# Macaron block with routed experts: combine weights gathered with the token rows, lists of token numbers only, expert 0's positions first, constants made early

## The reference, cut to what matters

```python
probs = softmax(xf @ router_w.T)                # 8192 tokens, 8 experts
topw, topi = top_k(probs, 2)
topw = topw / (topw.sum(-1, keepdims=True) + 1e-06)
# each expert keeps the 1280 tokens of its own with the largest weight (capacity)
order = lexsort((-fw, fe)); rank = arange(N * K) - starts[se]; keep = rank < capacity
g, u = disp @ wg, disp @ wu                     # per expert, 256 x 1024
eo = (silu(g) * u) @ wd                         # per expert, 1024 x 256
out = zeros.at[st].add(eo_of_the_token * (sw * keep))
x = x + 0.5 * mixture(layernorm(x))
```

## Time and profile before

| | |
|---|---|
| median of 3 runs | 1907.24 us (1907.22 to 1910.83) |
| the profiled execution's own time | 1911.83 us |
| its span, first to last instruction | 1910.1 us |
| TensorE matmul busy | 1622.9 us, 85% of the span |
| VectorE, ScalarE, GpSimd busy | 64%, 46%, 45% |
| mean granted TensorE clock | 0.937 |

### The profile page before, as it was taken

One profiled execution on the slowest core, in us unless ns is written; L12 is line 12 of the kernel. 1 busy time (PEld: TensorE's weight loads), 2 busy tenths in 40 slices (PEclk: granted clock), 3 DMA queues, 4 the chain that ended last, 5 costly groups with the idle time before them and its releaser, 6 DMA issues.

```text
span 1910.1 us, 40320 instructions
## 1 busy us (share of the span) xinstructions
PE 1622.9 (85%) x13943; PEld 1278.3 (67%) x13943; DVE 1231.0 (64%) x2915; ACT 886.9 (46%) x1627; POOL 869.0 (45%) x636
## 2 busy tenths in 40 slices
PE   4512999999999999986899751299999999999998
PEld 4411787877878788763577641168787787878876
DVE  8886748566485766526798887664745647465551
ACT  5521544445454454525565551144544545545452
POOL 5714163544626355136676651326254452635513
PEclk9999999999999999995899755589999999999999
DMA  6731261524516153126666450136062441615312
GB/s 220 261 133 40 83 128 41 129 53 95 120 29 148 32 116 66 18 42 166 143 146 146 139 197 0 28 95 127 28 143 47 102 105 43 132 39 125 61 23 28
DMA packets 261236, 182.16 MB, mean 95 GB/s; under 512 B 160938, under 2 KB 247860, under 8 KB 261172
## 3 DMA queue, kind: packets, MB, share of 16 engines
q1 hardware_dynamic: 230452, 139.37, 26.8%
q0 software_dynamic: 30720, 41.96, 13.3%
HBM read 89.01 MB, written 54.53 MB: 75 GB/s over the span
## 4 chain that ended last, share of the span: by engine, by line
PE 72%; DVE 12%; issue 6%; POOL 4%; DMA 2%; ACT 2%; SPq 0%; DVEq 0%; POOLq 0%; ACTq 0%
PE bank L1459 43%; PE bank L1472 22%; PE bank L1440 3%; POOL rstd L419 1%; DVE kT L1040 1%; DVE rT L1040 1%; POOL rows L423 1%; PE bank L1420 1%; PE bank L1504 1%; DVE gat L1249 1%; ACT xn L779 1%; DMA xs<-in_L_attn_x 1%; DVE v L1243 1%; DVE xn L944 1%; POOL hot_v L390 1%
## 5 line engine op out<-in xcount | busy, mean ns | idle before, releaser
L1459 PE MATMUL bank<-xT,w_g 128*128 128x320 f16 x3072 | 503.3, 300 | 31.4 <-DMA xT<-gat 31.4
L1115 DVE SCALAR_TENSOR_TENSOR unit_buf<-bank,sc_cur,unit_buf 128x320 f32<-128x320 f32 x512 | 281.6, 550 | 355.0 <-PE bank L1459 228.3
L1459 PE MATMUL bank<-xT,w_u 128*128 128x320 f16 x3072 | 503.3, 300 | 0.0
L721 ACT ACTIVATE unit_buf<-bank,sc_cur 128x320 f32<-128x320 f32 x512 | 269.5, 526 | 408.4 <-PE bank L1459 407.0
L1472 PE MATMUL bank<-w_d,xs 128*128 128x256 f16 x3840 | 423.8, 273 | 0.0
L1472 PEld LDWEIGHTS bank<-w_d,xs 128*128 128x128 f16 x3840 | 375.2, 98 | 44.4
L1459 PEld LDWEIGHTS bank<-xT,w_g 128*128 128x128 f16 x3072 | 295.6, 99 | 141.6 <-issue 31.9
L390 POOL TENSOR_TENSOR hot_v<-hot_b,val 128x400 bf16<-128x400 bf16 x128 | 147.7, 1154 | 520.8 <-DVE hot_b L1098 520.8
L1459 PEld LDWEIGHTS bank<-xT,w_u 128*128 128x128 f16 x3072 | 301.5, 98 | 118.1
L396 POOL DMA_INDIRECT gat<-rows_d,id_next x160 | 179.7, 1123 | 200.4 <-DVE id_next L1108 140.0
L1121 DVE TENSOR_TENSOR xs<-unit_buf,xs 128x320 f16<-128x320 f32 x512 | 268.4, 524 | 2.2
(11 more groups left out here) (230 smaller groups left out, 1811.9 us busy)
## 6 DMA issues: line engine op xcount, KB each, us to landing
rows_d<-rows SPq DMA_DIRECT2D x32, 512.0 KB, 3.4
raw_gu<-in_L_ffn_wg SPq DMA_DIRECT2D x16, 1024.0 KB, 5.6
raw_gu<-in_L_ffn_wu SPq DMA_DIRECT2D x16, 1024.0 KB, 9.1
raw_d<-in_L_ffn_wd SPq DMA_DIRECT2D x16, 1024.0 KB, 5.5
x_d<-xs SPq DMA_DIRECT2D x1, 8192.0 KB, 32.6
out_x<-xs SPq DMA_DIRECT2D x16, 512.0 KB, 3.5
xs<-in_L_attn_x SPq DMA_DIRECT2D x7, 1024.0 KB, 5.7
xs<-x_d SPq DMA_DIRECT2D x5, 1024.0 KB, 6.1
```

Source lines behind the costliest of these rows:

```text
L721: act.activation(act_s[:, u % 2, :], bank[u % 2][:, 0:CW], ACT.Silu, scale=sc_cur[:, 3:4]).then_inc(S.s_ready, 1)
L1115: dve.scalar_tensor_tensor(h32[:, u % HB, :], bank[2 + u % 2][:, 0:CW], sc_cur[:, 4:5], act_s[:, u % 2, :], mult, mult).then_inc(S.h32_rea ...
L1459: mm = pe.matmul(bank[2 * m + u % 2][:, 0:CW], wgu[m][:, w, k, f * P:(f + 1) * P], xT[:, a * KD + k, c * CW:(c + 1) * CW], start=(j == 0 a ...
```

## The change

- `rows_d` gets rows of 264 f32 numbers (1056 bytes) in place of 512 f16 numbers (1024 bytes): the 256 words of the two halves, and the token's 8 combine weights behind them. SyncE writes the weights from `wT` in four transfers as soon as both parts of `top_two` are done. GpSimd waits for them before the first gather. The routing works on a copy of its own, `wS`.
- `val` holds two values (tile plus 1, and partition), so `hot_v` has 20 columns in place of 50. GpSimd's five operations that split the weight are gone.
- `list_read` makes the token numbers from the two sums in two operations, and `w_next` only says whether a place is taken. `w_fac` multiplies it with the gathered weight, a column that is picked by the expert's number.
- `positions` replaces lines 1087 to 1091. It takes three operations in f32 and is run for expert 0 ahead of its list, and for experts 1 to 7 behind expert 0's `list_read`.
- For expert 0 VectorE makes `hot_v` itself.
- The constants are made by GpSimd at the start of the program.

```diff
-            def routing_constants():
-                gs.mark(pool.iota(slot_a[:, :, :], [[1, P], [0, LT]], base=0, channel_multiplier=0, **small))
...
+            gs.mark(pool.iota(slot_a[:, :, :], [[1, P], [0, LT]], base=0, channel_multiplier=0, **small))
+            gs.mark(pool.iota(slot_b[:, :], [[P, ST]], base=P, channel_multiplier=0, **small))
+            gs.mark(pool.iota(val[:, :, 0], [[1, NT]], base=1, channel_multiplier=0, **small))
+            gs.mark(pool.iota(val[:, :, 1], [[0, NT]], base=0, channel_multiplier=1, **small))
...
-                pool.tensor_tensor(hot_v[:, r], bc(hot_b[:, r], 2, 5), bc(vv, 3, ST), mult).then_inc(S.hot_v_ready, 1)
+                pool.tensor_tensor(hot_v[:, r], bc(hot_b[:, r], 2, 2), bc(val[:, at, :], 3, ST), mult).then_inc(S.hot_v_ready, 1)
...
-                parts = [val[:, :, :, 2 + k].rearrange("p e t -> p t e") for k in range(3)]
-                pool.wait_ge(S.w_ready, 2)
-                ch.step(pool.tensor_tensor(t3[:, :, :], t1[:, :, :], t2[:, :, :], mult))
-                ch.step(pool.tensor_copy(parts[0], t3[:, :, :]))
-                ch.step(pool.tensor_tensor(lg[:, :, :], t3[:, :, :], parts[0], sub))
-                ch.step(pool.tensor_copy(parts[1], lg[:, :, :]))
-                ch.step(pool.tensor_tensor(parts[2], lg[:, :, :], parts[1], sub))
-                for i in range(LP):
-                    list_piece(S, 0, i)
                 for stored in (S.stored0, S.stored1):
-                    pool.wait_ge(stored, 16 + 16 * STEPS)
+                    pool.wait_ge(stored, 16 + 16 * STEPS + (16 * G4 if stored is S.stored0 else 0))
                 gather(S, 0)
...
             def experts(S):
+                sp.wait_ge(S.w_ready, 2)
+                for g in range(G4):
+                    sp.dma_start(weights_v[:, g], wT[:, g * P:(g + 1) * P].rearrange(
+                        "p (c w) -> p c w", w=E)).then_inc(S.stored0, 16)
                 turn_rows(S, 0)
...
                 dve.wait_ge(S.back_turned, 1)
-                dve.wait_ge(S.pstep, 3)
-                vi, ai = t2[:, :, :].bitcast(i32), t3[:, :, :].bitcast(i32)
-                ch.step(dve.tensor_scalar(vi.rearrange("p t e -> p (t e)"), bank[5][:, :], float(P - 1), None, add))
-                ch.step(dve.tensor_scalar(ai, vi, P - 1, None, ALU.bitwise_and))
-                ch.mark(dve.tensor_copy(pos_a[:, :, :].rearrange("p e t -> p t e"), ai))
-                ch.step(dve.tensor_scalar(vi, vi, 7, None, ALU.logical_shift_right))
-                ch.step(dve.tensor_copy(pos_b[:, :, :].rearrange("p e t -> p t e"), vi))
+                positions(ch, 0, 1)
+
+            def positions(ch, e, n):
+                t, p = pos_i[:, :].unsqueeze(2) if n == 1 else t2[:, :, 0:n], pos_b[:, e:e + n, :].rearrange("p e t -> p t e")
+                back = bank[5][:, :].rearrange("p (t e) -> p t e", e=E)[:, :, e:e + n]
+                ch.step(dve.tensor_scalar(t, back, 1.0 / P, ROUND, mult, add))
+                ch.step(dve.tensor_scalar(p, t, ROUND, float(P), sub, mult))
+                ch.step(dve.scalar_tensor_tensor(pos_a[:, e:e + n, :].rearrange("p e t -> p t e"), back, HALF, p, add, sub))
...
+                if isinstance(n, int) and n == 0:
+                    dve.wait_ge(S.hot_b_ready, i + 1)
+                    dve.tensor_tensor(hot_v[:, r], bc(hot_b[:, r], 2, 2), bc(val[:, at, :], 3, ST),
+                                      mult).then_inc(S.hot_v_ready, 1)
 
             def list_read(S, ch, n):
                 dve.wait_ge(S.piece_used, LP * n + LP + 2)
-                ch.step(dve.tensor_copy(lst[:, :], bank[6][:, 0:5 * ST]))
-                ch.mark(dve.tensor_tensor(w_tmp[:, :], lst[:, 2 * ST:3 * ST], lst[:, 3 * ST:4 * ST], add))
-                ch.wait()
-                ch.mark(dve.tensor_tensor(w_next[:, :], w_tmp[:, :], lst[:, 4 * ST:5 * ST], add))
-                dve.scalar_tensor_tensor(id_next[:, :], lst[:, 0:ST], float(P), lst[:, ST:2 * ST], mult,
+                ch.step(dve.tensor_scalar(w_tmp[:, :], bank[6][:, 0:ST], 1.0, float(P), ALU.max, mult))
+                dve.scalar_tensor_tensor(id_next[:, :], bank[6][:, ST:2 * ST], -float(P), w_tmp[:, :], add,
                                          add).then_inc(S.ids_ready, 1)
+                ch.mark(dve.tensor_scalar(w_next[:, :], bank[6][:, 0:ST], 1.0, 0.5 / (HSHIFT * XSCALE), ALU.min, mult))
...
-                        dve.tensor_scalar(w_fac[:, :], w_next[:, :], sc_cur[:, 5:6], 0.5 / (HSHIFT * XSCALE), mult,
-                                          mult).then_inc(S.wfac_ready, 1)
+                        kept = gat_w[:, :, D + e] if isinstance(e, int) else gat_w[:, :, bass.ds(e + D, 1)][:, :, 0]
+                        dve.scalar_tensor_tensor(w_fac[:, :], kept, sc_cur[:, 5:6], w_next[:, :], mult,
+                                                 mult).then_inc(S.wfac_ready, 1)
...
                 list_read(S, ch, 0)
+                positions(ch, 1, E - 1)
...
-                    last = pe.matmul(bank[6][:, 0:5 * ST], hot_a[:, i % 2, :, t],
+                    last = pe.matmul(bank[6][:, 0:2 * ST], hot_a[:, i % 2, :, t],
```

More of the change, by code:

```diff
@@ L120, in macaron_block @@
         pos_b = sb("pos_b", [P, E, NT], b16)
-        val = sb("val", [P, E, NT, 5], b16)
+        val = sb("val", [P, NT, 2], b16)
+        pos_i = sb("pos_i", [P, NT], f32)
         hot_a = sb("hot_a", [P, 2, P, LT], b16)
         hot_b = sb("hot_b", [P, 2, LT, ST], b16)
-        hot_v = sb("hot_v", [P, 2, LT, 5, ST], b16)
+        hot_v = sb("hot_v", [P, 2, LT, 2, ST], b16)
         id_next = sb("id_next", [P, ST], u32)
@@ new lines, in _ @@
+            gs.mark(pool.iota(slot_a[:, :, :], [[1, P], [0, LT]], base=0, channel_multiplier=0, **small))
+            gs.mark(pool.iota(slot_b[:, :], [[P, ST]], base=P, channel_multiplier=0, **small))
+            gs.mark(pool.iota(val[:, :, 0], [[1, NT]], base=1, channel_multiplier=0, **small))
+            gs.mark(pool.iota(val[:, :, 1], [[0, NT]], base=0, channel_multiplier=1, **small))
+            for r in range(ROUNDS):
+                gs.mark(pool.memset(digit_f[:, r:r + 1], 4.0 ** (ROUNDS - 1 - r)))
@@ new lines, in _ @@
+            gs.mark(pool.memset(digit_f[:, ROUNDS:], 0.0))
+            gs.step(pool.iota(cand_f[:, :, :], [[0, ROUNDS + 1], [1, 4]], base=0, channel_multiplier=0, **small))
+            gs.step(pool.tensor_tensor(cand_f[:, :, :], cand_f[:, :, :], bc(digit_f[:, :], 2, 4), mult))
+            gs.mark(pool.tensor_copy(cand_i[:, :, :], cand_f[:, :, :]))
+            pool.wait_ge(s_boot, 2)
+            gs.step(pool.affine_select(out=before_e[:, :], in_=same_e[:, :], compare_op=ALU.is_gt, fill=0.0, base=0,
+                                       pattern=[[1, P]], channel_multiplier=-1))
@@ L1174, in ffn @@
                 with dve.Fori(0, E - 1) as e:
-                    ch.enter(e, 3 + 1 + 3 + (0 if S.scaled else 12 + 4))
+                    ch.enter(e, 3 + 1 + 2 + (0 if S.scaled else 12 + 4))
                     expert(S, ch, e, False)
```

47 lines of the change are left out of this document (25 added, 22 removed).

## The result

| | before | after |
|---|---|---|
| median on one chip | 1909.03 us (1907.22 to 1912.28, 4 runs) | 1885.89 us (1884.04 to 1887.99, 4 runs) |
| profiled execution, span | 1911.83, 1910.1 us | 1884.52, 1882.8 us |
| GpSimd, VectorE busy | 869.0, 1231.0 us | 795.8, 1194.2 us |

The ratio is 0.9877, with a 95% interval of 0.9857 to 0.9898: 23.1 us less.

A forecast was written before the change was run, and what follows sets the result against it. TensorE was taken to bound the experts, and a VectorE, GpSimd and SyncE chain the routings. Gains of 11.3 and 10.1 us, less 0.5 for stores, give 20.9, so 1907.24 becomes 1886.3 us; range 1877 to 1898.

The forecast's parts named there:

- constants: First routing's `top_two`: constants made early no longer slow line 1007; gain 1.2 us, once.
- stalls in the first rounds: Each mixture's first routing rounds: without GpSimd's weight split, VectorE's stalls go; gain 4.7 us, bounds 3.0 and 4.8.
- positions of expert 0: Turned places to first `hot_b`: three operations on 64 columns replace five on 512; gain 3.3 us per mixture.
- pieces of expert 0: Expert 0's list: eight pieces, all three operations on VectorE, period 1.14 us; gain 2.9 us, bounds 1.5 and 3.4.
- reading the list: Line 1104 to `id_next`: two operations and a wait take 0.4 us instead of 0.70; gain 0.3.
- loss in the gathers: Behind `id_next`: VectorE's shifted splits and positions slow GpSimd's gathers; loss 1.0 us per mixture, bounds 0 and 2.
- an instruction that is slow as the first of its kind: Rival for the first rounds: line 1027's stall is not GpSimd's, 4.7 us lost twice, 1896 us; chance 0.04.
- a gather takes more than 1.4 us: Sign, in the gathers behind `id_next`: a gather above this length would show the prediction wrong.
- the wider rows: Rival: rows of 1056 bytes lengthen each gather from 1.31 to up to 2.3 us, 1898 us; chance 0.08.
- Weights' transfers: SyncE's queue before the first gather: 8192 pieces stay hidden; rival of landing late, 1911 us, chance 0.05.
- Stores: `ffn_in` stores of wider rows: 0.5 us lost in all; rival of 0.35 us per pair, 1892 us, chance 0.05.
- Inside the experts: List pieces: 20 columns instead of 50 gain 0; rival that narrow matmuls count, 31 us, 1855, chance 0.05.

The follow-up runs named there:

- experiment 5: Changed kernel with the routing constants, in their new smaller form, back behind the first mixture's last quad; 1942.6 us.
- Experiment 4: Changed kernel with GpSimd's five weight-split operations back under the first rounds, on a spare buffer, result unused; 1969.0 us.
- Experiment 3: Changed kernel with the positions of all eight experts made ahead of expert 0's pieces, none behind; 1962.3 us.
- experiment 1: Changed kernel with the positions of experts 1 to 7 behind the four weight splits instead of ahead of them; 1953.8 us.
- experiment 11: The kernel before, unaltered, run again on the fourth chip; 1905.0 us.
- experiments 6 and 7: Changed kernel, from expert 1 on: first with list matmul weights in a row, 1971.3 us; then with 20 columns streamed three times, 1941.6 us.
- experiment 12: Changed kernel with weights in pairs from expert 1 on and other experts' positions behind the splits; 1858.8 us, ratio 0.9739 to the kernel before.
- experiment 10: Changed kernel with weights in a row from expert 1 on, written by eight short comparisons; 1942.9 us, ratio 0.9813 to the kernel before.

## Why the prediction was right, step by step

| step | predicted, us | measured, us |
|---|---|---|
| constants | 1.2, once | 1.40, once |
| stalls in the first rounds | 4.7 | 2.97 + 1.75 = 4.7 |
| positions of expert 0 | 3.3 | 3.39 |
| pieces of expert 0 | 2.9 (1.5 to 3.4) | 3.51 |
| reading the list | 0.3 | 0.32 |
| loss in the gathers | 1.0 (0 to 2) | 1.37 and 1.15 |
| sum of these rows, first and second mixture | 11.3 and 10.1 | 12.0 and 10.8 |
| the stretch, up to the end of the first experts | 11.3 | 12.2 |
| the stretch, from the second `top_two` to the end | 10.1 | 11.7 |
| both stretches | 21.4 | 23.9 |

- **Constants**: the size was nearly right, the reason only half. I credited the early place; experiment 5 shows that the smaller fills alone give all but 0.15. The early place alone might have done the same, which was not run. The 0.2 that I missed are lines 1010 and 1011, 0.63 and 0.29 us in the first `top_two` before and 0.56 and 0.20 now, where I had read all else as alike. The cover at the start held: GpSimd is done at 7.57 and its first power begins at 8.26, with 0.69 us to spare where I had 1.
- **Stalls**: the term that I could only infer from coincident ends. Experiment 4 gives 4.7 back to the tenth, in both mixtures, so they come from GpSimd's work and not from an instruction that is slow as the first of its kind. The Trainium skill (SBUF — State Buffer, Who interferes with whom) has copies and `tensor_scalar` among the instructions that take a port pair shared with GpSimd, and has the one that issues second wait for the other's whole instruction, while reductions don't. The copy and line 1037, which stalled, are of the first kind, and the reductions beside `slot_a` in experiment 5, which didn't, of the second. Copies and `tensor_scalar`s are not all that stalled: the third excess is a `scalar_tensor_tensor` (1.71 us for 0.22 in experiment 4), and line 993 is a `tensor_tensor`.
- **Positions**: right, and mainly through the order. I had put it to three operations on 64 columns in place of five on 512. Experiment 3 shows that the 64 columns do it: on 512 the new formula is 0.4 slower. Its share on 64 is at most 0.4, by the estimate there.
- **Pieces**: mis-sized by 0.6, just over its upper bound. `hot_v` was right (0.31 for 0.30), but in the pipelined chain it adds 0.24, not 0.30, and `hot_b` only 0.15. The period is 0.99 where I added whole lengths to 1.14; the tail was 0.4 longer than I had it. By my own sum the lower bound should have been 1.3 and not 1.5 (seven periods of 1.34 and a tail of 1.66).
- **Gathers**: the loss was inside its bounds, but its form was not as I told it. The condition "a gather takes more than 1.4 us" did occur, in two of ten. It was a poor sign, since one took 1.76 already before. And it was not the wider rows: seven of the others take 1.01 to 1.03 and the first its old 1.29, and experiment 1 shortens the stretch with rows as wide. Of it 0.3 to 1.1 us reach TensorE in the first mixture: from the end of `id_next` to TensorE's next list piece it takes 34.1 us, where the kernel before has 32.9 and, in experiment 11, 33.7. In the second it can't be read: that stretch takes 34.9, and the kernel before has 35.0 and 32.6.
- **Weights' transfers**: hidden by far. Nothing waits for them.
- **Stores**: ScalarE's wait went from 6.6 to 7.0 us in the first `ffn_in`, inside the 0.5 that I took, and `top_two` begins at 72.31 where it began at 72.29.
- **Inside the experts**: right. The gap stayed at 0.45, and experiments 6 and 7 show why: the load's stride costs, the columns don't. The Trainium skill (TensorE: Matmul & The Clock Gate, Back-to-back issue gap) has one price of 25 ns for 1 to 64 columns. Weights in a row and in pairs come to it (0.19 / 8 = 24 ns); with a stride of eight elements it is 56 ns, and the measurement decides.

The rows sum to 22.8 us and the two stretches to 23.9; the medians are 23.1 apart, the profiled executions 27.3. What the second stretch has beyond its rows, 0.9 us, lies behind `id_next`, in the part that varies by 2.5 us between two executions of the kernel before. Of the 27.3, 3.4 lie between the first experts and the second `top_two` (278.4 to 275.0), which the change hardly touches. The unaltered kernel before of experiment 11 has 273.3 there. So this is the variation of a run, not a gain.

That the median came within 0.4 us of the forecast is luck in part. The saving was 2.2 us short (20.9 for 23.1), and the median before, once its fourth run was in, stood 1.8 higher than the one that I subtracted from.

What stays open: why the change is worth 36 us on chips whose down projections wait, and what those wait for. The changed kernel was not run on the chip of experiment 12.

## What to carry to other kernels

When GpSimd works beside a chain of VectorE's operations, look for instructions that are three to twelve times longer than others of their shape and lie beside GpSimd's. Taking GpSimd's work out is then worth time even if nothing waits for its result: here 4.7 us for some 10 us of GpSimd's. Look through the whole chain for it: line 993 was missed. When a serial chain needs only the first of eight results, make that one alone first, and count what the rest does to the gathers that it now pushes other work under. When narrow matmuls take more than their columns ask, look at the stride of their weights, and find the layout that costs the writer least: pairs were enough here. When a change leaves the total alike, compare the stages one by one: in experiment 10 a loss of 12 us in one mixture hid a gain of 13 in the other.

## What the runs showed of the hardware that I had not expected

- The weight load of 128x128 bf16 takes 165 ns (mean) with elements eight apart, and 96 or 97 with elements two apart or in a row. Eight such matmuls of 20 columns take 0.45 and 0.19 us.
- VectorE's comparison of 1024 bf16 elements takes 0.68 us with runs of eight neighbours, 1.09 with runs of two, and 1.99 with one operand held still over 128 and the other read eight elements apart.
- A GpSimd product of 128x160 beside them takes 0.84, 1.25 and 2.15 us in the same order, and 0.47 beside `tensor_scalar`s of 128 columns.
- A gather's issue goes from 1.01 to up to 2.09 us beside VectorE's splits, though not beside each of them (1.01 at 166.46), and not beside line 1089, which reads PSUM and SBUF.
- A `tensor_tensor` of 128x384 f32 takes 2.46 us beside a `tensor_tensor` of GpSimd's, and operations of its shape 0.56 elsewhere.
- Of the four chips of the experiments, three took 71 to 87 us longer for the same kernel (1979 to 1995 against 1907). For the changed kernel, 49 of the 59 us are waits in front of the evictions of the down projections, at a granted clock of 0.937 against 0.944.
